# Four places for the parts of weighed rows, and an earlier addition of group sums in the second pass

## The reference

```python
x = x + L0(h)   # h_rel[src, type16] * norm, summed over the edges of each target
x = x + L1(h)   # Chebyshev, K = 3: Tx1 = prop(h), Tx2 = 2*prop(Tx1) - h, three 32x32 products, relu
x = x + L2(h)   # attention messages with 86 relations, summed by target, relu
x = x + L3(h)   # mean of h[src] over the edges of each target

def prop(v):    # inside L1
    return segment_sum(w_hat[:, None] * v[src], dst)
```

## Time and profile before

| | |
|---|---|
| median of 3 runs | 7698.59 us (7696.14 to 7699.79) |
| the profiled execution | 7688.82 us, span of its instructions 7687.0 us |
| mean granted TensorE clock | 0.644 of full speed |
| busy share of the span | PE 63%, PEld 54%, DVE 59%, ACT 31%, POOL 68% |
| pass 1, about | 2323 to 3418 us of the span |
| pass 2, about | 3465 to 4704 us |
| pass 4, about | 6940 to 7600 us |

### The profile page before, as it was taken

The page is one execution under the profiler, slowest core; times in us unless marked ns, Lnnn a source line. Parts: engine busy times, 40 slices in busy tenths (PEclk is TensorE's granted clock), DMA queues, the critical chain, the costliest instruction groups (busy, mean ns, idle before and its releaser), DMA issues. The chain is left out here.

```text
span 7687.0 us, 150121 instructions
## 1 busy us (share of the span) xinstructions
PE 4849.7 (63%) x41375; PEld 4128.6 (54%) x41376; DVE 4540.0 (59%) x14144; ACT 2349.6 (31%) x7420; POOL 5231.6 (68%) x5417
## 2 busy tenths in 40 slices
PE   5333333333336767776777775777777777786777
PEld 2222222222225555565666665777777777775667
DVE  5555555557778888875555553444444444447776
ACT  4444444440002222213545454111112111123222
POOL 2777777777756777757666662777777777756663
PEclk8655555555556666668888786555555555558998
DMA  7000000000004444436888887222222222216554
GB/s 173 14 14 14 14 14 14 14 14 13 13 12 122 128 128 126 129 103 189 293 276 293 272 293 231 41 41 41 41 41 41 41 41 41 41 34 162 154 162 116
DMA packets 539741, 757.13 MB, mean 98 GB/s; under 512 B 226073, under 2 KB 382265, under 8 KB 539509
## 3 DMA queue, kind: packets, MB, share of 16 engines
q1 hardware_dynamic: 309893, 395.03, 16.9%
q0 software_dynamic: 173168, 146.14, 12.1%
q10 hardware_dynamic: 56448, 213.62, 7.2%
HBM read 424.12 MB, written 330.21 MB: 98 GB/s over the span
## 5 line engine op out<-in xcount | busy, mean ns | idle before, releaser
L790 POOL DMA_INDIRECT arena<-table,ibuf x3328 | 3150.1, 947 | 1241.7 <-issue 1125.7
L790 POOL DMA_INDIRECT arena<-nodes,ibuf x2080 | 2078.8, 999 | 1070.7 <-issue 616.8
L1190 PE MATMUL ps_agg<-mem_a,arena 128*32 128x80 f32 (+1 forms) x3744 | 470.0, 307 | 555.6 <-DVEq L1643 506.9
L1190 PE MATMUL ps_agg<-mem_b,arena 128*32 128x80 f32 (+1 forms) x3744 | 473.5, 308 | 511.4 <-DVEq L1643 498.0
L1190 PEld LDWEIGHTS ps_agg<-mem_a,arena 128*32 128x32 f32 (+1 forms) x3744 | 411.2, 155 | 615.2 <-DVEq L1643 524.8
L1190 PEld LDWEIGHTS ps_agg<-mem_b,arena 128*32 128x32 f32 (+1 forms) x3744 | 413.8, 156 | 560.8 <-DVEq L1643 521.4
L1459 PE MATMUL ps_agg<-tbuf,msg 128*64 128x80 f32 x2496 | 373.6, 344 | 330.6 <-DVE msg L2128 330.6
L1061 ACT ACTIVATE att<-score 128x8 f32<-128x8 f32 x208 | 43.3, 208 | 1649.5 <-DVE score L2119 1649.5
L1459 PEld LDWEIGHTS ps_agg<-tbuf,msg 128*64 128x64 f32 x2496 | 336.1, 227 | 351.7 <-DVE msg L2128 351.7
L913 ACT ACTIVATE tbuf<-O,tbuf 128x49 bf16<-128x49 bf16 x1664 | 448.7, 363 | 79.2 <-DVE H L1810 79.2
L1888 DVE TENSOR_SCALAR tbuf<-idx_a,pcol 128x768 bf16<-128x768 bf16 (+1 forms) x1040 | 397.3, 425 | 109.5 <-issue 53.6
(11 more groups left out here) (392 smaller groups left out, 12081.6 us busy)
## 6 DMA issues: line engine op xcount, KB each, us to landing
table<-tbuf ACTq DMA_DIRECT2D x294, 544.5 KB
idx_a<-lows_d SPq DMA_DIRECT2D x637, 192.0 KB
targets_d<-tbuf SPq DMA_DIRECT2D x182, 384.0 KB
H<-targets_d SPq DMA_DIRECT2D x182, 384.0 KB
arena<-table,ibuf POOLq DMA_INDIRECT x3328, 2.5
table<-tbuf ACTq DMA_DIRECT2D x98, 495.0 KB
O<-targets_d SPq DMA_DIRECT2D x91, 384.0 KB
arena<-nodes,ibuf POOLq DMA_INDIRECT x2080
```

Source lines behind the costliest of these rows:

```text
L790: nc.gpsimd.indirect_dma_start(out=INTO[s][:, k, c, 0:WIDTH[s]], out_offset=None, in_=TABLE[s], in_offset=bass.IndirectOffsetOnAxis(ap=ibu ...
L1190: last = nc.tensor.matmul(ps_agg[ROW0[s]:ROW0[s] + CHN[s], 0:WIN], narrow[:, k, c, 0:CHN[s]], onehots[b][:, c, :], start=(c == 0), stop=(c ...
```

## The change

`slot_rows` gets four places, used in turn (`q % 4`): the old one in `mem_a`, a shorter one in `mem_b` (six columns), and two in a new buffer `more_rows` of 576 columns. Every reader and writer takes `q % 4` in place of `b`. ScalarE's wait ahead of the high part of batch `q` is for the `send` of batch `q - 4` instead of `q - 2`, in the passes 1, 2 and 4.

In pass 1 VectorE's step is reordered: `weigh_group` keeps its step (1, 3, 5, 7), but `add_group` of the same group is one step earlier (2, 4, 6 and 0 of the next turn), so that no step holds both. Both stand ahead of `add_block`, and the drain at the end of the even steps is gone. Pass 2 keeps its order.

```diff
+        more_rows = sb("more_rows", [P, 576])
+        slot_rows = [m.bitcast(BF16).rearrange("p (k c) -> p k c", c=SPLIT)
+                     for m in (mem_a[:, 640:976], mem_b[:, 640:928], more_rows[:, 0:288], more_rows[:, 288:576])]
...
-                            act.wait_ge(s_sent, at + 1)
+                            if (BEFORE[h] + f) * NBATCH + q > 1:
+                                act.wait_ge(s_sent, at - 1)
                             act.wait_ge(s_wgh, at + 1)
                             carry_wait(act)
-                            nc.scalar.copy(slot_rows[b][:, 0:n, 0:D], ...).then_inc(s_high, 1)
+                            nc.scalar.copy(slot_rows[q % 4][:, 0:n, 0:D], ...).then_inc(s_high, 1)
...
                         act.wait_ge(s_got, at + 3)
-                        act.wait_ge(s_sent, at + 1)
+                        act.wait_ge(s_sent, at - 1)
...
+                        if s == 1:
+                            if q - 1 in HIDDEN[s]:
+                                weigh_group(s, i, HIDDEN[s][q - 1], f=f)
+                            if q - 2 in HIDDEN[s]:
+                                add_group(s, i, HIDDEN[s][q - 2], f)
+                            if q == 0 and not first:
+                                add_group(s, i, SLOTS - 1, f - 1)
                         if q % NBATCH == 2 and (q >= NBATCH or not first):
                             add_block(i, f + q // NBATCH - 1)
-                        if q - 3 in HIDDEN[s]:
-                            add_group(s, i, HIDDEN[s][q - 3], f)
-                        if q == 1 and not first:
-                            add_group(s, i, SLOTS - 1, f - 1)
-                        if q - 1 in HIDDEN[s]:
-                            weigh_group(s, i, HIDDEN[s][q - 1], f=f)
-                        else:
-                            dve.drain()
+                        if s == 2:
+                            if q - 3 in HIDDEN[s]:
+                                add_group(s, i, HIDDEN[s][q - 3], f)
+                            if q == 1 and not first:
+                                add_group(s, i, SLOTS - 1, f - 1)
+                            if q - 1 in HIDDEN[s]:
+                                weigh_group(s, i, HIDDEN[s][q - 1], f=f)
+                            else:
+                                dve.drain()
```

More of the change, by code:

```diff
@@ L965, in pick_weighed @@
                             n, b = BATCHES[q][1], q % 2
-                            act.wait_ge(s_sent, at + 1)
+                            if (BEFORE[h] + f) * NBATCH + q > 1:
+                                act.wait_ge(s_sent, at - 1)
                             act.wait_ge(s_wgh, at + 1)
                             carry_wait(act)
-                            nc.scalar.copy(slot_rows[b][:, 0:n, 0:D], by_tile(weighed[b][:, 0:n * D])).then_inc(s_high, 1)
+                            nc.scalar.copy(slot_rows[q % 4][:, 0:n, 0:D], by_tile(weighed[b][:, 0:n * D])).then_inc(s_high, 1)
                         if goes(q - 1):
@@ L972, in pick_weighed @@
                             act.wait_ge(s_rest, at)
-                            nc.scalar.copy(slot_rows[b][:, 0:n, D:2 * D], by_tile(rest[b][:, 0:n * D])).then_inc(s_mid, 1)
+                            nc.scalar.copy(slot_rows[(q - 1) % 4][:, 0:n, D:2 * D], by_tile(rest[b][:, 0:n * D])).then_inc(s_mid, 1)
                         if s == 1:
@@ L997, in pick_block @@
                         act.wait_ge(s_got, at + 3)
-                        act.wait_ge(s_sent, at + 1)
+                        act.wait_ge(s_sent, at - 1)
                         carry_wait(act)
-                        nc.scalar.copy(slot_rows[b][:, 0:n, :], picked_rows(b)[:, 0:n, 0:SPLIT]).then_inc(s_slot, 1)
+                        nc.scalar.copy(slot_rows[q % 4][:, 0:n, :], picked_rows(b)[:, 0:n, 0:SPLIT]).then_inc(s_slot, 1)
                         if q in HIDDEN4[e]:
@@ L1320, in send @@
                     for k in range(n):
-                        last = nc.tensor.matmul(block_sums[s][0:SPLIT, 0:W2], slot_rows[q % 2][:, k, :], to_oh[s][q % TO_RING[s]][:, k, :],
+                        last = nc.tensor.matmul(block_sums[s][0:SPLIT, 0:W2], slot_rows[q % 4][:, k, :], to_oh[s][q % TO_RING[s]][:, k, :],
                                                 start=(b0 + k == 0), stop=(b0 + k == NBK - 1))
@@ L1953, in pick_weighed @@
                             V.tensor_tensor(by_tile(rest[b][:, 0:n * D]), by_tile(weighed[b][:, 0:n * D]),
-                                            slot_rows[b][:, 0:n, 0:D], ALU.subtract).then_inc(s_rest, 1)
+                                            slot_rows[(q - 1) % 4][:, 0:n, 0:D], ALU.subtract).then_inc(s_rest, 1)
                         if goes(q - 2):
@@ L1957, in pick_weighed @@
                             dve.wait_ge(s_mid, count(i, f, q, -1))
[L1958 to L1959 removed]
+                            V.tensor_tensor(slot_rows[(q - 2) % 4][:, 0:n, 2 * D:SPLIT], by_tile(rest[b][:, 0:n * D]),
+                                            slot_rows[(q - 2) % 4][:, 0:n, D:2 * D], ALU.subtract).then_inc(s_slot, 1)
+                        if s == 1:
[5 more added lines that the diff above has]
+                                add_group(s, i, SLOTS - 1, f - 1)
                         if q % NBATCH == 2 and (q >= NBATCH or not first):
                             add_block(i, f + q // NBATCH - 1)
[L1962 to L1969 removed]
+                        if s == 2:
[7 more added lines that the diff above has]
+                                dve.drain()
                         if s == 2 and q % 4 == 2 and (q >= 6 or not first) and q < NBATCH + 4:
```

1 line of the change is left out of this document (removed).

## The result

The changed kernel takes **7615.74 us** (median of 4 runs, 7609.18 to 7627.45); the kernel before took 7697.36 us beside it (7692.76 to 7699.79). The profiled execution took 7618.78 us (span 7617.0).

A forecast was written before the change was run, and what follows sets the result against it. GpSimd's DMA issuing was taken to bound pass 1, and a circle of waits through TensorE and VectorE pass 2. Gains of 70 us (pass 2) and 1 us (pass 1) took 7698.6 to 7628 us, range 7580 to 7685.

The forecast's parts named there:

- TensorE's wait for `ht`: Pass 2, TensorE's section of each half-turn: this wait of 1.07 us goes wholly, over 46.5 half-turns.
- The odd high part: Pass 2, VectorE's section: its wait for odd batches' high part, 1.2 us a half-turn, shrinks by 0.8 us.
- The deduction of a fifth for the DMA engines: Pass 2: fuller DMA queues lose part of the gain, so 88 us was cut to 70 us.
- No wait of L1953 over 0.5 us: Pass 2, sign of being right: none of VectorE's waits for a high part stays above 0.5 us.
- The new wait of 0.8 us for the multiplication: Pass 2: the group addition moves up until it waits about 0.8 us for the multiplication's end, inside TensorE's section.
- GpSimd's 41.7 covers that: Pass 1: GpSimd's DMA issuing, 41.7 us a turn, sets the pace and hides VectorE's changes; gain 1 us.
- the prediction's own bound of 5 us: Pass 1: the prediction calls itself wrong if this pass changes by more than 5 us.
- the slower rival: Pass 1: VectorE's even steps wait w us behind TensorE's multiplication, costing 26 x (4w - 1.2); 7753 us at w = 1.5; chance 0.06.
- A pass 2 bound by the DMA engines: Rival, pass 2: DMA engines limit it, leaving about 1.5 us a turn, 35 us, total 7664; chance 0.12.
- a wait that only moves: Rival, pass 2: VectorE's and TensorE's waits turn into others; some 5 us gained in all, 7694; chance 0.10.
- the case of 0.90: Rival, pass 2: TensorE's mean clock grant rises from 0.81 to 0.90, a further 37 us, total 7591; chance 0.13.
- GpSimd was not stretched: Rival, pass 1: VectorE's two-port work stretches GpSimd more, losing 50 us of the gain, total 7678; chance 0.04.

The follow-up runs named there:

- ht_first: Kernel before, two places, with ScalarE's copy of the turned pair moved ahead of the waiting high part in pass 2: 7632.43 us, ratio 0.9923.
- alloc_only: Kernel before with the new buffer allocated and used by nothing: 7693.32 us, ratio 1.0004.

## Why the prediction was right in its total, and where it failed

**What bounds pass 2: right.** The wait of 161.7 us was not the gain: ht_first left its even part as it was and took 49 us off the pass. The prediction gave 46.5 x 1.07 = 50 us to TensorE's wait for `ht`. Spread over all 38 half-turns the wait is 1.01 us, so this should have been 47. That ht_first measured 49 is in part luck, since it halved the odd wait as well. In the changed kernel the wait for `ht` lost 29.4 us in 19 turns; over the 23.3 turns of the pass that is an estimated 36 us.

**The odd high part: mis-sized.** 0.8 of 1.2 us a half-turn, 37 us before the deduction, were counted because the high part would be "ready just when VectorE wants it". It is not: it waits behind piece 0, and its wait is 36.8 us in 19 turns, 0.97 us a half-turn, where 45.8 us were 1.2. By its own wait it gave 0.24 us a half-turn, an estimated 11 us. The deduction of a fifth for the DMA engines hid more than half of this error: 70 us predicted, 57 measured in the mean. "No wait of L1953 over 0.5 us" failed: the even batches still have 58.1 us in 34 waits, up to 3.3. A share of 0.91 was reached, not over 0.92, and ScalarE's 42.7 us of waiting for the table's stores is where the full queues show. The new wait of 0.8 us for the multiplication came to 4.9 us in 19 turns. The turn of 44 to 45 us came out at 45.0. The Trainium skill, "DMA: Bandwidth & Descriptors", Specifications, has about 358 GB/s as the limit of memory for a core. These 19 turns moved 302, so nothing here tests it.

**Pass 1, "GpSimd's 41.7 covers that": failed.** By the prediction's own bound of 5 us it was wrong here. Two sizes were right: the group sum's wait is 33.1 us over 104 even steps, w = 0.32 us where 0.15 to 0.4 were said, and the odd steps fell by 0.77 us each where 0.7 was said. The even steps grew by 0.9 us in the mean where 0.4 to 0.6 were said, most of it in step 2, so VectorE's turn grew by 0.6 us and did not shrink. And there was no cover. VectorE's turn was as long as GpSimd's because it was nearly the bound itself; it went from waiting for a landing to 4.1 us behind the earlier trace rows, and that growing lag was the sign that I read as slack. Two bounds of equal length didn't hide each other's growth here. Step 2 was the second miss: I let the slack in front of the next weighing absorb the block's 0.8 us, but the copy comes a further 0.84 us late behind the group sum (mean 0.91 us in 25 times), and TensorE's wait for it rose from 13.1 to 54.3 us. This is the mechanism of the slower rival, at 12 us and not the 71 from which it decides. "At most 1.2 us that the order saves" against 4w = 1.3 was its sum, and the block was missing in it.

**Pass 4: right on the change, wrong on the result.** The wait there costs nothing, as said (761 and 764 us). The 35 us came from a thing that was on no list, the place of the loop's code. The 2.99 us ahead of L1912 were in the trace of before, but no row of the prediction read them.

**The rivals.** A pass 2 bound by the DMA engines (35 us in all) and a wait that only moves (5 us) are excluded by 57. TensorE's clock rose only from 0.81 to 0.85 in pass 2, and ht_first with its 49 us has 0.83; the case of 0.90 did not come. alloc_only has 0.85 as well (3704 to 4607 us) and still 1343 us for the pass, so a step of 0.04 went with 5 us at most there. GpSimd was not stretched but eased: 979 ns for a DMA against 999.

The sum: -57 + 12 - 35 = -80 us, against -71. That it was close is luck: what pass 4 gave covered what passes 1 and 2 lacked.

## What to carry to other kernels

Two engines of equal turn length covered nothing for each other here: read the lag between them at the start and at the end of a loop, and where it grows, count every added wait of the later one in full. A long wait is worth only what the next wait behind it leaves; here a copy moved one place up in ScalarE's list gave 49 us where twice the buffers gave 57. After an edit ahead of a long loop, compare the loop's idle time of issue before and after, and try the edit with padding that never runs before its gain is put down to the edit.

## What the runs showed of the hardware that was not expected

- 112 instructions that never run took 37 us away (764 to 727 us in pass 4), and 16 that run once in a microsecond or so put 40 us back (725 to 765). Pass 4 took 725 to 730 us in four kernels and 760 to 765 in six, the source of the loop the same but for the wait that costs nothing, with a stall of some 3 us in ten of 13 turns ahead of one copy of VectorE, or without it. Each of these 60 stalls holds an instruction packet of 8192 bytes, and the copy starts 1.61 to 1.77 us after it.
- On one chip every kernel took 1.37 to 1.40 times as long, with gaps of 1.8 to 2.6 us between TensorE's matmuls, waits of VectorE that no record explains, and an unchanged duration of VectorE's comparison (421 and 424 ns). There the new order alone gains 147 us in pass 1 where it loses 12 elsewhere.
- GpSimd's indirect DMAs in pass 1 took 978 to 981 ns in the four kernels with the new order and 999 to 1002 in the six with the old one; why was not tried.
